# Local attention on blocks of 64 queries with their own 128 keys, on four 64x64 tiles of TensorE, in units of four heads

## The chip, the cores and the metric

The kernel runs on one core of one Trainium2 chip. The metric is the device time of the one launch in microseconds (us), from the first to the last instruction and what lies around them. PE is TensorE, PEld its weight loads, DVE is VectorE, ACT is ScalarE, POOL is GpSimd, SP is SyncE. PSUM is the memory that PE writes; it has 8 banks of 512 fp32 columns.

## The reference, cut to what matters

The model is a chain of stages over x of shape (2, 512, 128): a conditioned block (A, M), a quantised attention (B), a causal attention with an image key (C), and last a two-layer transformer (`_L0_ffn_ref`). Only the last has local attention, and only that is touched. Each of its 2 layers does, for 2 batches of 512 tokens, 8 heads of 64 channels and a window of 64:

```python
q = l2norm(q) * qs; k = l2norm(k) * ksc
q, k = rotary_xpos(q, k)
# local attention, w = n // 64 blocks of 64 queries, each with the keys of its own block and of the one before
bq = q.reshape(b, h, w, 64, d) * 8.0
bk, bv = look_around(bk), look_around(bv)          # (b, h, w, 128, d)
sim = einsum('bhwid,bhwjd->bhwij', bq, bk)
mask = (i < j) | (i > j + 64) | (j == -1)
attn = softmax(where(mask, -max, sim))
out = einsum('bhwij,bhwjd->bhwid', attn, bv)
x = x + out @ wo
```

After it come a shifted layer norm and a gated feed-forward part.

## The kernel before, in words

Everything is written out by hand in `build`, one program per engine, with named semaphores; the order of each engine's instructions is the order in the code, and there is no planner. Tokens are held in T = 8 tiles of 128 rows (TB = 4 per batch b). For each layer l the three projections are made tile by tile into `qkvD` (L1730, copied by ACT at L625). DVE takes the norms (L1209) and does the rotary part (`rope_terms`), for batch 0 ahead of the attention and for batch 1 inside the attention of batch 0: the generator `late_rope` (L1285 to L1290, and the scaling at L300) gives one piece of it in each unit of batch 0. `turn_qk(b)` (L1745) transposes q and k of one batch in 32 fp32 transposes; ACT (L619) and DVE (L278) copy them to `qTD` and `kTD`.

The attention itself goes in units of two heads (one `pair`) of one tile of 128 queries: 16 units per batch, 32 per layer, 64 in all. The 128 queries need up to 192 keys (the 64 before the tile, and its own 128), in a batch's first tile 128. A unit passes through the engines in this order:

- S on PE: two fp32 matmuls of 64x128 weights (the queries) and 192 columns (the keys), one for each head, in two row tiles (L1784), and on top of them two bf16 matmuls that add the mask (L1787). Each fp32 matmul is two instructions in the trace, and each fp32 transpose is one. The scores lie in banks 0 and 1 or 6 and 7.
- DVE: the negated maximum of both heads (`s_nmD`, L1319), its product with the scale (`s_nbD`, L1323), and, one unit behind, the reciprocal of the sums (`s_rsD`, L1332).
- ACT: one exponential per head with its sum (L653, two instructions each in the trace) into `prob_d(U)`, one of four buffers in `sq` and `dev`.
- POOL: both heads' probabilities times the reciprocals (L417).
- PE: four fp32 transposes of 128x128 (two in the first tile), L1803, two units behind S. The 64 columns of the first key tile that a query tile can't reach hold zeros, written once (L1222).
- ACT: the transposed probabilities copied to `probTD` (L666), also two units behind.
- PE: the product with the values, per head and key tile one fp32 matmul of 128x64 weights (values) and 128 columns, in two column tiles (L1820), three units behind S.
- DVE: `put_o`, once per tile, copies the output (L828).

PE's order in a unit u is S(u), transposes (u-2), values (u-3). S(u) waits until the exponentials of unit u-2 have left its banks. In batch 1 PE also runs `project_o` for the four tiles of batch 0 (L1753), one in each of its first four units, and `shift_rows` in unit 7; DVE runs `add_o` (unit 4), `receive` (7), `less_mean` (8) and `variance` (10), the layer norm of batch 0. At the seam between the batches PE runs `turn_qk(1)`.

## Time and profile before

| | |
|---|---|
| median of 3 runs | 843.0 us (842.24 to 846.91) |
| the profiled execution | 843.34 us, its span 841.4 us |
| mean granted TensorE clock | 0.813 |
| PE busy | 673.9 us (80%), 4514 instructions |
| DVE busy | 588.3 us (70%) |
| ACT busy | 520.9 us (62%) |
| POOL busy | 237.2 us (28%) |

An engine's busy share is a mean over stages with different limits, and matmuls overlap, so a busy PE is not PE at its peak. The granted clock is 1.0 at 2.4 GHz and 0.5 at 1.2 GHz. The four stretches of local attention (layer 0 and 1, batch 0 and 1) are the part to read: 555.5 to 594, 600 to 641, 716 to 754 and 760 to 801 us of the span.

### The profile page before, as it was taken

The page shows a single profiled execution, that of the slowest core. Times are in us where ns is not written, and L with a number is a line of the kernel's source. Part 1 is how long each engine was busy: PE and PEld are TensorE (multiplying, and loading weights), DVE is VectorE, ACT ScalarE, POOL GpSimd, SP SyncE. Part 2 cuts the span into 40 slices and gives each one's busy share as a digit, 9 for nine tenths or more (in the row PEclk, how much of TensorE's full clock was granted, in tenths as well). Part 3 has the DMA queues.
Part 4 walks back from the last instruction along what each step waited for, and adds up shares of the span by engine and source line. Part 5 has one row for each costly group of instructions (what it writes and reads, how often), then busy time and mean ns, then how long its engine had stood idle before and what let it go on. Part 6 is the DMA issues. An engine that isn't in the chain of part 4 may idle for free.

```text
span 841.4 us, 12993 instructions
## 1 busy us (share of the span) xinstructions
PE 673.9 (80%) x4514; PEld 406.8 (48%) x4514; DVE 588.3 (70%) x1285; ACT 520.9 (62%) x1237; POOL 237.2 (28%) x233
## 2 busy tenths in 40 slices
PE   6679976776889889858887887677898695779867
PEld 2322232542556556645554554254656543456545
DVE  7882348368998897577787764998454669874564
ACT  4479977654778777144776673745575475565742
POOL 5030040013889789512000000026231000452300
PEclk9689986888555555656999998969999797699998
DMA  9400000000000000000000000000000000000000
GB/s 296 142 1 1 2 2 0 1 0 1 1 2 1 1 2 1 1 0 1 1 2 1 2 2 0 1 0 1 2 2 1 0 1 1 0 2 1 1 1 25
DMA packets 9059, 10.54 MB, mean 13 GB/s; under 512 B 2746, under 2 KB 7844, under 8 KB 8868
## 3 DMA queue, kind: packets, MB, share of 16 engines
q1 hardware_dynamic: 8996, 9.73, 3.5%
q8 instruction: 36, 0.59, 0.3%
q14 instruction: 27, 0.22, 0.1%
HBM read 9.21 MB, written 0.52 MB: 12 GB/s over the span
## 4 chain that ended last, share of the span: by engine, by line
PE 45%; DVE 33%; ACT 9%; issue 8%; POOL 3%; DMA 0%; DVEq 0%; ACTq 0%; POOLq 0%
PE ps L1398 4%; PE ps L1561 4%; PE ps L1658 4%; DVE s_nmB L1040 3%; PE ps L1548 3%; PE ps L1641 3%; PE ps L1678 2%; DVE s_nmD L1319 2%; PE ps L1820 2%; PE ps L1803 2%; ACT arena L522 2%; PE ps L1839 2%; PE ps L1753 2%; PE ps L1469 2%; PE ps L1784 2%
## 5 line engine op out<-in xcount | busy, mean ns | idle before, releaser
L382 POOL TENSOR_SCALAR arena<-arena,s_rB,s_zpu 128x512 uint8<-128x512 f32 x128 | 115.9, 943 | 42.3 <-DVE s_rB L1013 41.5
L417 POOL TENSOR_TENSOR sq<-sq,s_rsD 128x384 f32<-128x384 f32 (+1 forms) x32 | 35.4, 1105 | 296.0 <-DVE s_rsD L1332 296.0
L560 ACT ACTIVATE arena<-ps,s_nmB 128x512 f32<-128x512 f32 x128 | 86.6, 683 | 31.4 <-DVE s_nmB L1040 30.8
L582 ACT ACTIVATE arena<-ps,s_nmx 128x512 f32<-128x512 f32 (+3 forms) x128 | 60.7, 527 | 49.7 <-DVE s_nmx L1138 49.3
L1040 DVE TENSOR_REDUCE s_nmB<-ps 128x2 f32<-128x1024 f32 x64 | 77.4, 1218 | 6.6 <-PE ps L1548 6.2
L1133 DVE TENSOR_REDUCE s_nmx<-ps 128x1 f32<-128x512 f32 (+3 forms) x128 | 56.6, 484 | 20.5 <-PE ps L1644 20.0
L522 ACT ACTIVATE arena<-ps 128x1024 f32<-128x1024 f32 x64 | 60.9, 1026 | 5.8 <-PE ps L1453 5.8
L1561 PE MATMUL ps<-cst,arena 128*128 128x128 f32 x256 | 61.9, 421 | 1.2 <-ACT arena L552 0.8
L1404 PE MATMUL ps<-ones 128*128 128x512 f16 x134 | 43.5, 488 | 22.2 <-ACT s_wn L493 6.6
L1319 DVE TENSOR_REDUCE s_nmD<-ps 128x2 f32<-128x384 f32 (+1 forms) x64 | 33.5, 524 | 39.1 <-PE ps L1787 28.9
L1561 PEld LDWEIGHTS ps<-cst,arena 128*128 128x128 f32 x256 | 49.3, 221 | 14.4 <-POOL arena L382 7.9
L1548 PE MATMUL ps<-staged 8*128 8x512 f16 x128 | 45.8, 580 | 12.4 <-ACT arena L560 11.5
L1658 PE MATMUL ps<-cst,arena 128*128 128x128 f32 x320 | 47.6, 303 | 8.6 <-issue 5.3
L653 ACT ACTIVATE sq<-ps,s_nbD,s_dq 128x192 f32<-128x192 f32 (+1 forms) x64 | 31.3, 493 | 32.3 <-DVE s_nbD L1323 32.3
L653 ACT ACTIVATE dev<-ps,s_nbD,s_dq 128x192 f32<-128x192 f32 (+1 forms) x64 | 31.3, 494 | 24.6 <-DVE s_nbD L1323 24.6
L1658 PEld LDWEIGHTS ps<-cst,arena 128*128 128x128 f32 x320 | 40.1, 157 | 11.8 <-issue 11.2
L417 POOL TENSOR_TENSOR dev<-dev,s_rsD 128x384 f32<-128x384 f32 (+1 forms) x32 | 32.3, 1010 | 47.2 <-DVE s_rsD L1332 47.2
L1730 PE MATMUL ps<-w_d,uT 128*128 128x512 f32 x96 | 42.3, 595 | 3.5 <-ACT uT L472 2.7
L1784 PE MATMUL ps<-arena 64*128 64x192 f32 (+1 forms) x256 | 39.7, 390 | 4.1 <-ACT sq L653 2.3
L1820 PE MATMUL ps<-arena 128*64 128x128 f32 x448 | 40.4, 296 | 1.7 <-ACT arena L666 1.4
L1641 PE MATMUL ps<-staged 51*128 51x512 bf16 (+3 forms) x128 | 32.7, 329 | 10.2 <-ACT arena L582 9.0
L1404 PEld LDWEIGHTS ps<-ones 128*128 128x128 f16 x134 | 14.8, 118 | 49.0 <-issue 13.0
(344 smaller groups left out, 1562.3 us busy)
## 6 DMA issues: line engine op xcount, KB each, us to landing
vec<-in_vec SPq DMA_DIRECT2D x1, 1882.0 KB, 11.9
w_d<-in_wqkv SPq DMA_DIRECT2D x2, 768.0 KB
vec<-in_vec SPq DMA_DIRECT2D x1, 960.0 KB, 8.3
w_h<-in_w SPq DMA_DIRECT2D x2, 341.0 KB
x_tok<-in_x SPq DMA_DIRECT2D x1, 512.0 KB, 4.1
arena<-in_w_f SPq DMA_DIRECT2D x2, 256.0 KB, 7.9
rope<-in_rope SPq DMA_DIRECT2D x1, 512.0 KB, 10.4
w_do<-in_wo SPq DMA_DIRECT2D x2, 256.0 KB
```

Source lines behind the costliest of these rows:

```text
L382: nc.gpsimd.tensor_scalar(u8[:, n % 4, j // 2, :, 2 * (j % 2)], prob[:, n % 2, j * 512:j * 512 + 512], sm("rB", 8)[:, c:c + 1], sm("zpu", ...
L417: nc.gpsimd.tensor_tensor(pr, pr, per_row(rs, 256 - k0), ALU.mult).then_inc(sem["normD"], 1)
L522: nc.scalar.activation(prob[:, n % 2, half * 1024:half * 1024 + 1024], ps[:, 2 * half:2 * half + 2, :], ACT.Exp, scale=HD ** -0.5).then_in ...
L560: nc.scalar.activation(prob[:, n % 2, j * 512:j * 512 + 512], ps[:, j, :], ACT.Exp, bias=sm("nmB", 8)[:, c:c + 1], accum_out=sm("sumB", 8) ...
L582: nc.scalar.activation(probC[:, n % 2, at(qt):at(qt) + w], ps[:, bank, col:col + w], ACT.Exp, bias=nmx[:, TB * b + qt, h:h + 1]).then_inc( ...
L653: nc.scalar.activation(prob_d(U)[:, j, k0:256], ps[:, 6 * (u % 2) + j, k0:256], ACT.Exp, scale=sm("dq8", 8 * T)[:, h:h + 1], bias=sm("nbD" ...
L1040: free(V.tensor_reduce(sm("nmB", 8)[:, c:c + 2], ps[:, 2 * half:2 * half + 2, :], X, ALU.max, negate=True), "maxB")
L1404: M(ps[:, 5, :], ones16[:, :], ones16[:, 0:1].to_broadcast([P, 512]), start=True, stop=True)
L1548: ins = M(ps[:, j, :], staged[r, G % 2, qt * P:qt * P + P], staged[r, G % 2, 512:1024], start=True, stop=True)
L1561: ins = nc.tensor.transpose(ps[:, 4 + i, c:c + P], codes[:, m % 4, i, c:c + P], ident)
L1641: M(o, stb[r, G % 2, qt * P:qt * P + P], stb[r, G % 2, 512:512 + w], start=(qt > 0), stop=False)
L1658: ins = nc.tensor.transpose(ps[:, 3 + bank, c:c + P], probC[:, n % 2, a:a + P], ident)
```

## The change

A unit is now four heads (two pairs) of one tile of 128 queries: 8 units per batch, 32 in all. Each half of the tile (64 queries) meets only its own 128 keys: the second half the keys of the tile, the first half the tile's first 64 keys and, in columns 64 to 127, the 64 keys before the tile. So each head has one square of 128x128 probabilities, and all of its rows are written.

- S: two bf16 mask matmuls of 256 columns come first, then eight fp32 matmuls of 64x64 weights and 128 columns, on four tiles of 64x64 (head j by half). In a batch's first tile the first half has 64 columns.
- DVE: one maximum, one product and one reciprocal per unit of four heads, over 4x128 columns. In batch 0 `late_rope` gives two pieces per unit, one before and one after the reciprocal.
- ACT: four exponentials of 128 columns, one copy of 512 columns.
- POOL: one product of 128x512, and a new step `mixed_values(l, t)` ahead of each tile: rows 0 to 63 of the tile's values, and rows 64 to 127 of the values of the tile before (not in a batch's first tile), are copied to the tile's q region of `qkvD`, which is dead by then. These are the weights for the first half.
- PE: four transposes, then eight fp32 matmuls of 128x64 weights and 64 columns for the values. A new wait on `mixD` stands ahead of them.
- `put_o`, `add_o`, `receive`, `less_mean`, `variance`, `squares_d` and `shift_rows` sit at other units; `project_o` runs for two tiles in each of the first two units of batch 1. The zeroing at L1222 is gone, and the mask table is another.

```diff
+                def s_d(b, u):
+                    t = TB * b + u // 2
+                    m = P * (u % (2 * TB) < 2)
+                    for j in range(2):
+                        M(ps[:, 6 * (u % 2) + j, 0:256], identb[:, :], dmask[:, m:m + P].unsqueeze(1).to_broadcast([P, 2, P]),
+                          start=True, stop=False)
+                    for a in range(2):
+                        for half in range(2):
+                            for j in range(2):
+                                r, pair = slice(64 * j, 64 * j + 64), 2 * (u % 2) + a
+                                q = qTD[r, pair, t * P + WINDOW * half:t * P + WINDOW * half + WINDOW]
+                                o = scores_d(u)[WINDOW * half:WINDOW * half + WINDOW, j, a, :]
+                                k = kTD[r, pair, t * P:t * P + P]
+                                if half == 0 and t % TB == 0:
+                                    o, k = o[:, 0:WINDOW], k[:, 0:WINDOW]
+                                elif half == 0:
+                                    k = kTD[r, pair, t * P - WINDOW:t * P + WINDOW].rearrange("p (n c) -> p n c", c=WINDOW)[:, ::-1, :]
+                                ins = M(o, q, k, start=False, stop=(a == 1))
+                    ins.then_inc(sem["sD"], 1)
+                def pv_d(t, v):
+                    for half in range(2):
+                        rows = slice(0, WINDOW if half == 0 and t % TB == 0 else P)
+                        for a in range(2):
+                            for j in range(2):
+                                pair, c = 2 * (v % 2) + a, P * (2 * j + a) + WINDOW * half
+                                values = 2 * INNER * half + DHD * (2 * pair + j)
+                                o = P * pair + WINDOW * half
+                                ins = M(ps[64 * j:64 * j + 64, 4 + t % 2, o:o + WINDOW], qkvD[rows, t, values:values + DHD],
+                                        probTD[rows, v % 2, c:c + WINDOW], start=True, stop=True)
+                    ins.then_inc(sem["pvD"], 1)
...
                         if u < TB * 2:
                             if u >= 2:
-                                pe.wait_ge(sem["expD"], 2 * (U - 1))
+                                pe.wait_ge(sem["expD"], 4 * (U - 1))
+                            s_d(b, u)
-                        if b == 1 and u < TB:
-                            project_o(u)
+                        if b == 1 and u < TB // 2:
+                            project_o(2 * u)
+                            project_o(2 * u + 1)
...
+            def mixed_values(l, t):
+                b = t // TB
+                pool.wait_ge(sem["qkT_D"], 8 * (B * l + b) + 4)
+                if T * l + t:
+                    pool.wait_ge(sem["normD"], 2 * (T * l + t))
+                step(nc.gpsimd.tensor_copy(qkvD[0:WINDOW, t, 0:INNER], qkvD[0:WINDOW, t, 2 * INNER:3 * INNER]), "mixD")
+                if t % TB:
+                    step(nc.gpsimd.tensor_copy(qkvD[WINDOW:P, t, 0:INNER], qkvD[WINDOW:P, t - 1, 2 * INNER:3 * INNER]), "mixD")
+                    for u in range(TB * 2):
+                        U = T * 2 * l + TB * 2 * b + u
+                        if u % 2 == 0:
+                            mixed_values(l, TB * b + u // 2)
+                        pool.wait_ge(sem["ratesD"], U + 1)
+                        rs = sm("rsD", 16)[:, 4 * (U % 4):4 * (U % 4) + 4]
+                        nc.gpsimd.tensor_tensor(prob_d(U), prob_d(U), per_row(rs, P), ALU.mult).then_inc(sem["normD"], 1)
...
-                            for j in range(2):
-                                c = 2 * (U % 4) + j
+                            for k in range(4):
+                                j, a = divmod(k, 2)
+                                c = 4 * (U % 4) + k
+                                nc.scalar.activation(prob_d(U)[:, k, :], scores_d(u)[:, j, a, :], ACT.Exp,
...
+                            step(V.tensor_reduce(nm, scores_d(u), X, ALU.max, negate=True))
+                            free(V.tensor_tensor(nb, nm, dq8[:, hh:hh + 4].rearrange("p (a j) -> p j a", j=2), ALU.mult),
+                                 "maxD")
+                        if b == 0 and u < TB * 2:
+                            next(rest, None)
                         if u >= 1:
-                            dve.wait_ge(sem["expD"], 2 * U)
+                            dve.wait_ge(sem["expD"], 4 * U)
+                            free(V.reciprocal(sm("rsD", 16)[:, c:c + 4], sm("sumD", 16)[:, c:c + 4]), "ratesD")
-                        if b == 0 and u < TB * 4:
+                        if b == 0 and u < TB * 2:
                             next(rest, None)
...
+                            for k in range(4):
+                                ins = nc.tensor.transpose(ps[:, 2 + u % 2, P * k:P * k + P], prob_d(U - 2)[:, k, :], ident)
                             ins.then_inc(sem["ptD"], 1)
...
+                            pe.wait_ge(sem["mixD"], 2 * (T * l + t) - (B * l + b) + 1)
+                            pv_d(t, u - 3)
```

## Rows read from the trace of the kernel before

**Rows 1.** Windows: stretch, then each engine's busy us (instructions), then granted clock, DMA

```profile
555.50:594.00 38.50, 29.63 (x224) 17.50 (x224) 31.78 (x69) 22.37 (x74) 20.29 (x14) 0.87 0.00 1
600.00:641.00 41.00, 36.27 (x329) 24.24 (x328) 19.97 (x64) 27.20 (x85) 13.19 (x17) 1.00 0.01 2
760.00:801.00 41.00, 36.35 (x329) 24.33 (x328) 20.06 (x64) 27.13 (x85) 13.19 (x17) 1.00 0.00 1
```

**Rows 2.** Timeline, PE, batch 1 of layer 0: start us, us, what, [idle before]

```profile
629.72 0.66 PE L1820 MATMUL ps<-arena 128*64 128x128 f32 x8
630.31 0.59 PE L1784 MATMUL ps<-arena 64*128 64x192 f32 x4
630.84 0.34 PE L1787 MATMUL ps<-dmask,identb 128*128 128x192 bf16 x2
631.01 0.60 PE L1803 MATMUL ps<-cst,dev 128*128 128x128 f32 x4
631.54 0.66 PE L1820 MATMUL ps<-arena 128*64 128x128 f32 x8
```

**Rows 3.** Timeline, batch 0 of layer 0: a rotary piece beside POOL's product

```profile
579.72 1.21 DVE L1290 TENSOR_TENSOR arena<-o_tok,staged 128x1024 f32<-128x1024 f32 x1
579.88 1.73 POOL L417 TENSOR_TENSOR sq<-sq,s_rsD 128x384 f32<-128x384 f32 x1 [2.10 <-DVE s_rsD L1332]
```

**Rows 4.** Groups by line and shape, batch 0 of layer 0, DVE: pieces of `late_rope`

```profile
L1285 DVE TENSOR_TENSOR o_tok<-arena,ropeL 128x1024 f32<-128x1024 f32 x4 | 4.8, 1207 | 0.0
L1288 DVE TENSOR_TENSOR staged<-arena,ropeL 128x512 f32<-128x512 f32 x4 | 4.4, 1090 | 0.1
L1287 DVE TENSOR_TENSOR staged<-arena,ropeL 128x512 f32<-128x512 f32 x4 | 2.7, 672 | 0.0
```

**Rows 5.** Timeline, PE: four column tiles; sixteen short matmuls with loads; both from other stages

```profile
98.56 1.07 PE L1469 MATMUL ps<-arena 128*32 128x512 f32 x8
303.09 0.59 PE L1575 MATMUL ps<-arena 128*128 128x5 f16 x16
```

**Rows 6.** Timeline, DVE, ACT, POOL, batch 1 of layer 0: one unit behind its scores

```profile
633.04 0.56 DVE L1319 TENSOR_REDUCE s_nmD<-ps 128x2 f32<-128x384 f32 x1 [0.98 <-PE ps L1787]
633.83 0.51 ACT L653 ACTIVATE dev<-ps,s_nbD,s_dq 128x192 f32<-128x192 f32 x1 [0.24 <-DVE s_nbD L1323]
633.95 0.82 POOL L417 TENSOR_TENSOR sq<-sq,s_rsD 128x384 f32<-128x384 f32 x1 [0.99 <-DVE s_rsD L1332]
634.82 0.59 ACT L666 ACTIVATE arena<-ps 128x512 f32<-128x512 f32 x1
634.93 0.60 PE L1803 MATMUL ps<-cst,sq 128*128 128x128 f32 x4
635.13 0.56 DVE L1319 TENSOR_REDUCE s_nmD<-ps 128x2 f32<-128x384 f32 x1 [1.26 <-PE ps L1787]
```

**Rows 7.** Groups by line and shape: instructions' total us, mean ns, idle before

```profile
L1133 DVE TENSOR_REDUCE s_nmx<-ps 128x1 f32<-128x512 f32 x32 | 22.0, 686 | 2.4 <-PE ps L1644 1.9
L653 ACT ACTIVATE dev<-ps,s_nbD,s_dq 128x128 f32<-128x128 f32 x16 | 7.2, 452 | 6.2 <-DVE s_nbD L1323 6.2
L407 POOL COPY arena<-arena 128x512 f32<-128x512 f32 x2 | 1.9, 938 | 0.0
L417 POOL TENSOR_TENSOR sq<-sq,s_rsD 128x256 f32<-128x256 f32 x2 | 1.2, 612 | 6.4 <-DVE s_rsD L1332 6.4
```

**Rows 8.** Timeline: the seam, and the start and end of batch 1

```profile
595.79 3.71 PE L1745 MATMUL ps<-cst,arena 128*128 128x128 f32 x32 [0.95 <-ACT dev L653]
603.19 0.49 PE L1784 MATMUL ps<-arena 64*128 64x128 f32 x4
640.97 0.71 PE L1753 MATMUL ps<-w_do,arena 128*128 128x128 f32 x4 [0.79 <-DVE arena L828]
```

**Rows 9.** Windows: the stretch at half clock; turning alone ahead of layer 1's attention

```profile
560.40:570.60 10.20, 9.07 (x44) 4.73 (x44) 8.29 (x18) 5.24 (x20) 5.23 (x4) 0.50 0.00 1
708.00:716.00 8.00, 6.66 (x36) 6.46 (x36) 7.79 (x11) 3.32 (x6) 0.00 (x0) 0.63 0.01 2
```

More of the change, by code:

```diff
@@ L638, in _ @@
                 for b in range(B):
-                    for u in range(TB * 4 + 2):
-                        U = T * 4 * l + TB * 4 * b + u
-                        if u == TB * 4 and b == 0:
+                    for u in range(TB * 2 + 2):
+                        U = T * 2 * l + TB * 2 * b + u
+                        if u == TB * 2 and b == 0:
                             turned_qk(1)
-                        if u < TB * 4:
-                            t, pair = divmod(u, 4)
-                            first = t == 0
+                        if u < TB * 2:
                             act.wait_ge(sem["maxD"], U + 1)
@@ L1219, in factors @@
                        d_.rearrange("p (t k h) -> p t k h", t=TB, k=2)[:, :, 0, :], 8.0, ALU.mult, name="d_dn")
-                for a in (wide["sq"], wide["dev"]) if l == 0 else ():
-                    step(V.memset(a[:, :, :].rearrange("p t c -> p (t c)").rearrange("p (n k) -> p n k", k=256)[:, :, 0:WINDOW],
-                                  0.0), "outside")
                 for t in range(TB):
@@ L1304, in _ @@
                 for b in range(B):
-                    for u in range(TB * 4 + 1):
-                        U = T * 4 * l + TB * 4 * b + u
-                        if u == TB * 4 and b == 0:
+                    for u in range(TB * 2 + 1):
+                        U = T * 2 * l + TB * 2 * b + u
+                        if u == TB * 2 and b == 0:
                             for i in (1, 3, 5, 7):
                                 turned_qk(1, i)
-                        if u < TB * 4:
-                            t, pair = divmod(u, 4)
-                            k0 = P if t == 0 else WINDOW
+                        if u < TB * 2:
@@ L1334, in _ @@
+                        if b == 0 and u < TB * 2:
                             next(rest, None)
-                        if u >= 8 and u % 4 == 0:
-                            put_o(l, TB * b + u // 4 - 2)
-                        if b == 1 and u == 4:
+                        if u >= 5 and u % 2:
+                            put_o(l, TB * b + (u - 5) // 2)
+                        if b == 1 and u == 2:
                             add_o(0)
-                        if b == 1 and u == 8:
+                        if b == 1 and u == 6:
@@ L1340, in _ @@
                             less_mean(0)
-                        if b == 1 and u == 10:
+                        if b == 1 and u == 7:
                             variance(0)
+                    put_o(l, TB * b + TB - 2)
                     put_o(l, TB * b + TB - 1)
@@ L1769, in _ @@
                     pe.wait_ge(sem["qk_evV"], 4 * (B * l + b + 1))
-                    for u in range(TB * 4 + 3):
-                        U = T * 4 * l + TB * 4 * b + u
-                        if u == TB * 4 and b == 0:
-                            pe.wait_ge(sem["expD"], 2 * U)
+                    for u in range(TB * 2 + 3):
+                        U = T * 2 * l + TB * 2 * b + u
+                        if u == TB * 2 and b == 0:
+                            pe.wait_ge(sem["expD"], 4 * U)
@@ L1782, in _ @@
                                 shift_rows(0)
-                            for j in range(2):
-                                M(ps[:, 6 * (u % 2) + j, k0:256], qTD[64 * j:64 * j + 64, pair, t * P:(t + 1) * P],
-                                  kTD[64 * j:64 * j + 64, pair, (t - 1) * P + k0:(t + 1) * P], start=True, stop=False)
-                            for j in range(2):
-                                ins = M(ps[:, 6 * (u % 2) + j, k0:256], identb[:, :], dmask[:, k0:256],
-                                        start=False, stop=True)
@@ L1795, in _ @@
                             pe.wait_ge(sem["normD"], U - 1)
-                            if l == 0 and U < 4:
-                                pe.wait_ge(sem["outside"], 2)
                             if U >= 4:
                                 pe.wait_ge(sem["ptcD"], U - 3)
-                            for j in range(2):
-                                for k in ((1,) if first else (0, 1)):
-                                    c = 256 * j + P * k
-                                    ins = nc.tensor.transpose(ps[:, 2 + v % 2, c:c + P],
-                                                              prob_d(U - 2)[:, j, P * k:P * k + P], ident)
+                            for k in range(4):
+                                ins = nc.tensor.transpose(ps[:, 2 + u % 2, P * k:P * k + P], prob_d(U - 2)[:, k, :], ident)
@@ L1812, in _ @@
                                 pe.wait_ge(sem["o_D"], T * l + t - 1)
[L1813 removed]
+                            if u % 2 and t == TB + 1:
                                 pe.wait_ge(sem["do_ev"], B * l + 1)
[L1815 to L1822 removed]
```

82 lines of the change are left out of this document (24 added, 58 removed).

## The prediction

> **What bounds the kernel now.** I read the table of busy shares first; it names PE, but over all stages. So next the windows over the stretches the change touches. Batch 0 of layer 0 takes 38.5 us with PE busy for 29.6 and DVE for 31.8, batch 1 takes 41.0 us with PE busy for 36.3 and DVE for only 20.0 [rows 1]. Layer 1 repeats layer 0 (its batch 1 is the last line of [rows 1]), so each sum is made for layer 0 and doubled. The reader is to see two different limits, and the timeline shows both.
>
> In batch 1 PE runs unit after unit with hardly a gap: values 0.59 us from start to start, scores 0.53, mask 0.17, transposes 0.53, in all 1.82 us for two heads [rows 2]. PE sets the pace. In batch 0 DVE does the rotary part besides: four pieces each of L1285 (1.21), L1287 (0.67), L1288 (1.09) and of the addition at L1290 (1.21), and two scalings at L300, taken at the same 1.2, together 19.1 us [rows 3, 4]. POOL's product, 0.82 us alone, lasts 1.73 when it starts 0.16 us after such a piece [rows 3, 6]: it waits until the piece is over. DVE, POOL and PE take turns there.
>
> **PE's work for a unit of four heads.** 32 transposes of 128 columns take 3.71 us from first start to last end [rows 8], so one each 0.11 us. Four of them last 0.53 until the next kind starts [rows 2], which is 4 x 0.11 and 0.09 for the change to another tile shape. The value matmuls (eight instructions in two column tiles) take 0.59, which is four rounds of 0.11, 0.06 for the first weights and 0.09 for the change: two tiles do run beside each other. Scores are two rounds of 192 columns (0.16), the weights of 128 columns (0.11) and the change (0.09), 0.52.
> - Scores after: 16 instructions of 128 columns. If four tiles of 64x64 run beside each other it is four rounds of 0.11, 0.05 for weights, 0.09 for the change: 0.58. The trace before has no tile of 64 rows and 64 columns. The nearest is L1469, four column tiles of 32: eight instructions of 512 columns in 1.07 us, so only two rounds [rows 5]. Nothing overlapping would be 16 x 0.11 = 1.8 plus 0.14, 1.9; more overlap than one round for four isn't to be had. I take 0.58, and 1.9 for the range.
> - Values after: eight rounds of 64 columns, 0.055 each, 0.06 and 0.09: 0.59 against 2 x 0.59. 16 matmuls with their loads come out in 0.59 us, less the last one's 0.17 or so, that is 0.027 each [rows 5], so the issue of 16 takes 0.43 and doesn't slow the 0.44.
> - Mask: 2 x 256 columns at 0.107, and a change of tile shape ahead of the scores: 0.30. Transposes: four instead of eight, 0.53.
> The sum is 2.00 us instead of 3.64.
>
> A rule that speaks against the value part: the Trainium skill (TensorE: Matmul & The Clock Gate, Part 3, "The mechanism") says that a weight load overlaps a running matmul only where the row group differs. All value matmuls use all rows. By it each of eight loads of about 0.05 us would be exposed, 0.4 us a unit, and the result would be about 818 us. The row speaks against it: eight loads and eight passes fit in 0.59 us, of which the columns alone take 0.44 [rows 2].
>
> **The other engines, for four heads.** ACT: four exponentials of 128 columns, 0.45 each [rows 7], and one copy (0.59, the next starts 0.49 after): 2.3 us, before 4 x 0.49 and two copies, 2.9. DVE: the maximum of 512 columns costs 0.69 (L1133 [rows 7]) and the two small ones 0.08 each from start to start, with the gaps 0.91; before twice 0.75. POOL: 256 columns 0.61, 384 columns 0.82 [rows 6, 7], so 512 take 1.04. The mixed values are new: two copies of 64x512 per tile, one per unit. The nearest row is L407, 128x512 at 0.94 [rows 7]; the bounds are 0.4 (half of that, if fewer rows cost less) and 2.1 (0.94 and a whole rotary piece waited for). I take 0.94. The new wait on `mixD` stands on PE ahead of the values; behind it are the next scores. The copies end three units earlier, so it costs nothing.
>
> **Batch 1 after.** POOL needs 1.98 a unit, PE 2.00, ACT 2.3; none of them sets the pace, a round trip does. From a maximum to the first exponential 0.79 [rows 6], plus 0.13 for the longer maximum; four exponentials until the copy may start 1.79; the copy of the earlier unit 0.59 and 0.05; then PE values 0.59, mask 0.30, scores 0.49, and 0.20 until the maximum two units on starts (634.93 to 635.13 [rows 6]). That is 4.93 us for two units, 2.46 each. The trip over POOL is shorter: 1.04 to its start, 1.04 there, 0.05, transposes 0.53, then the same 1.58: 4.24. So what ends last moves from PE's columns to the copy that stands behind four exponentials in ACT's queue.
> Before, batch 1 runs from 603.19 to the projection at 640.97 [rows 8], 37.8 us. After: in each of the first two units scores (0.88) and 16 instructions for two tiles of `project_o` (16 x 0.11, 0.09), 2.75 each; the transposes of unit 0 start at 6.4, of unit 1 at 8.7, of unit 7 at 8.7 + 6 x 2.46 = 23.5; its copy, values and `put_o` end 2.8 later, 26.3. The layer norm of batch 0 on DVE and the shift on PE, now in half as many units, add 1.5. So 27.8 us, 10.0 less.
>
> **Batch 0 after.** DVE has 7 units of 0.91, the 19.1 us of rotary pieces (14 in 16 places, so they end in unit 6) and one `put_o` of 0.7: 26.2 us. The copies on POOL hold back a piece by some 0.4 each, as L1288 (1.09) is held against L1287 (0.67), the same size [rows 4]: 2.8. So 29.0 us for seven units, 4.1 each. The trip over POOL with a piece ahead of the reciprocal is 4.24 + 1.3 + up to 1.0 of waiting = 6.5 for two units at the full clock, some 8.4 at half clock, so it ties with DVE there. The first maximum is about 1.2 us after the start at 555.9; with the last exponentials (2.7) `turn_qk` starts at 589.0 instead of 595.79, 6.8 less. Against that stand longer units at the seam (0.5) and some loss to the clock (1.0). So 5.3 less. The zeroing at L1222 lay in DVE's idle time: 0.
>
> **Sum.** 2 x (10.0 + 5.3) = 30.6 us off the profiled execution's 843.34 (span 841.4), which is 0.3 over the median of 843.0: **813 us**.
>
> **Rivals.**
> 1. The clock. PE does less in batch 0: 2.0 us of work in 4.1. It was already at half clock (1.2 GHz) from 560.4 to 570.6, where it waited for DVE and POOL in the first units [rows 9], and at 2.4 GHz afterwards. If it stays at half for the whole of batch 0, a unit is about 4.5 us (2.5 more) and `turn_qk(1)` starts at half (2.5 more): 5 per layer, 823 us. For it: fewer columns in the same time. Against it: the work comes in dense bursts. The Trainium skill (TensorE: Matmul & The Clock Gate, Part 4) has it that transposes don't count as busy for the clock. The trace disagrees: PE ran transposes alone ahead of layer 1's attention, at a mean of 0.63 over 8 us [rows 9], so the clock rose on them. By the rule, the 2.0 us would count as only 1.5, and this rival would be the likelier; by the row I hold it back.
> 2. The four tiles don't all run together. In pairs the scores cost 0.44 more: 2 to 3 us per layer, 818. One after another 1.3: the trip is 3.1 a unit, 6 to 7 per layer, 826.
> 3. Slower. Each change between tiles of a different row and column drains, 0.11 + 0.09 for each of 16 passes: scores 3.2, PE 4.6 a unit. Batch 1 would take 8 x 4.6 and some 6, 43 us against 37.8, and batch 0, twice that slow in its half-clock part, about 10 more: 2 x 15, 873 us. It decides from the point where a unit costs 3.9 us in batch 1, that is scores of 2.5. Against it: pairs of row tiles and of column tiles run without a drain [rows 2].
> 4. Better. The copies on POOL fall where DVE reads PSUM and hold nothing back (2.5), and ACT's 2.3 sets batch 1 (1.3), with the seam and clock free (1.5): 5.3 per layer, 802.
>
> **How the numbers follow.** The forecast has 0.57, the clock 0.16, the tiles without overlap 0.12, slower 0.04, better 0.11. 813 is that of the likeliest. The range goes down to rival 4's 802 and a little past it, 801, and up to 829: past the clock (823) and serial tiles (826), and it holds the copies at 2.1 (about 2 per layer, 817); what is left out is rival 3, two rivals together, and a mis-sized trip. Faster by over 0.5% (about what a measurement tells from no change) 0.94, within it 0.02, slower 0.04.
>
> **What would show it.** In batch 1 a unit of 2.4 to 2.5 us, with the value matmuls waiting for ACT's copy (L666's successor) and PE idle for 0.4 of it; the sixteen score passes in 0.6 us; batch 1 of 28 us, batch 0 of 33. The first product on POOL about 1.04 alone, and a copy of mixed values near 0.9. Wrong would be: PE still without gaps in batch 1 (rival 2), a clock of 0.5 at the seam (rival 1), POOL as what transposes wait for in batch 1 (the copies cost more than 1.4), or stretches outside the attention that move by more than 1 us.

## The result, and the profile after

The changed kernel takes **817.8 us** (median of 4 runs, 816.6 to 818.8) against 843.3 for the kernel before on the same chip: a ratio of 0.9697 (95% interval 0.9664 to 0.9731), 25.5 us less. Forecast were 813 and 801 to 829. The profiled execution has a span of 816.3 us (841.4 before) and a mean granted clock of 0.780 (0.813 before). One run of e2 below (1021.1 us) was a slow one: e2's median of 809.3 counts it, its ratio does not, and the other five have a median of 808.2.

The windows show the three stretches of layer 0 that the prediction's sum is made of; the fourth line is a part of batch 1. Columns as in [rows 1].

```profile
557.50:590.20 32.70, 21.05 (x249) 13.77 (x249) 27.84 (x47) 18.31 (x71) 17.13 (x13) 0.68 0.01 2
590.20:599.60 9.40, 8.39 (x94) 7.50 (x98) 3.83 (x7) 3.97 (x7) 2.13 (x3) 0.85 0.01 2
599.60:630.00 30.40, 25.30 (x340) 18.65 (x341) 15.49 (x38) 20.84 (x75) 12.44 (x14) 0.89 0.01 1
610.10:616.90 6.80, 6.80 (x60) 4.65 (x58) 0.95 (x3) 4.01 (x16) 2.79 (x4) 0.50 0.00 0
```

The reader is to see the granted clock, the last number but two: 0.68, 0.85 and 0.89, where batch 0 stood at 0.87 and batch 1 at 1.00 before [rows 1]. In 6.8 us in the middle of batch 1 TensorE was busy without a break at half clock (1.2 GHz). The stretches at half clock are 562.3 to 582.8, 589.6 to 593.0 and 610.1 to 616.9; before, only 560.4 to 570.6 in this part of layer 0 [rows 9], and 720.8 to 734.5 in layer 1. In the changed kernel layer 1 has the same three: 709.1 to 729.6, 736.4 to 739.8, 756.9 to 763.7.

The timeline of PE in batch 1, first at full clock, then at half, then at full again (start, us, what, idle before and who ended it); it answers to [rows 2]:

```profile
604.80 0.38 PE L1774 MATMUL ps<-dmask,identb 128*128 128x256 bf16 x2
605.11 0.67 PE L1787 MATMUL ps<-arena 64*64 64x128 f32 x16
605.71 0.66 PE L1826 MATMUL ps<-cst,sq 128*128 128x128 f32 x4
...
608.00 0.66 PE L1826 MATMUL ps<-cst,sq 128*128 128x128 f32 x4 [0.82 <-POOL sq L431]
609.17 0.83 PE L1799 MATMUL ps<-arena 64*64 64x64 f32 x16 [0.52 <-ACT arena L675]
...
610.36 1.13 PE L1787 MATMUL ps<-arena 64*64 64x128 f32 x16
611.42 1.11 PE L1826 MATMUL ps<-cst,dev 128*128 128x128 f32 x4
612.46 1.32 PE L1799 MATMUL ps<-arena 64*64 64x64 f32 x16
...
617.57 0.69 PE L1799 MATMUL ps<-arena 128*64 128x64 f32 x16
618.19 0.39 PE L1774 MATMUL ps<-dmask,identb 128*128 128x256 bf16 x2
618.51 0.67 PE L1787 MATMUL ps<-arena 64*64 64x128 f32 x16
619.81 0.66 PE L1826 MATMUL ps<-cst,sq 128*128 128x128 f32 x4 [0.63 <-POOL sq L431]
620.92 0.69 PE L1799 MATMUL ps<-arena 128*64 128x64 f32 x16 [0.46 <-ACT arena L675]
```

Sixteen score passes take 0.60 us from their start to the next kind's (605.11 to 605.71), values 0.62 (617.57 to 618.19), the mask 0.31. At half clock the scores take 1.06 (610.36 to 611.42). Where [rows 2] has no gap, PE now waits: ahead of the transposes for Pool's product (0.82, 0.63, 0.57 and 0.21 us in batch 1), ahead of the values for ScalarE's copy (0.52, 0.46, 0.57 and 0.46).

The other sizes, by shape over 557 to 630 (count, total us, mean ns, idle before); they answer to [rows 6, 7]:

```profile
L1321 DVE TENSOR_REDUCE s_nmD<-ps 128x4 f32<-128x512 f32 x16 | 11.0, 690 | 13.8 <-PE ps L1787 7.3 <-ACT sq L665 3.7 <-issue 1.4
L675 ACT ACTIVATE arena<-ps 128x512 f32<-128x512 f32 x16 | 9.5, 601 | 3.0 <-PE ps L1826 3.0
L420 POOL COPY arena<-arena 64x512 f32<-64x512 f32 x7 | 5.7, 810 | 0.9
L422 POOL COPY arena<-arena 64x512 f32<-64x512 f32 x6 | 5.6, 933 | 0.4
```

And one copy of mixed values beside a rotary piece, with the product that follows it on Pool; the product at 604.15, in batch 1, is one by itself ([rows 3] has such a pair of before):

```profile
570.30 1.22 DVE L303 TENSOR_TENSOR arena<-o_tok,s_dn 128x1024 f32<-128x1024 f32 x1
570.41 1.58 POOL L420 COPY arena<-arena 64x512 f32<-64x512 f32 x1
572.05 1.50 POOL L422 COPY arena<-arena 64x512 f32<-64x512 f32 x1
573.62 1.04 POOL L431 TENSOR_TENSOR dev<-dev,s_rsD 128x512 f32<-128x512 f32 x1
...
604.15 1.04 POOL L431 TENSOR_TENSOR sq<-sq,s_rsD 128x512 f32<-128x512 f32 x1 [6.24 <-DVE s_rsD L1334]
```

The seam answers to [rows 8]: the turn of queries and keys, the first scores of batch 1, and the projection that ends it.

```profile
590.15 5.10 PE L1748 MATMUL ps<-cst,arena 128*128 128x128 f32 x32 [0.66 <-ACT dev L665]
...
599.19 0.39 PE L1774 MATMUL ps<-dmask,identb 128*128 128x256 bf16 x2
...
629.77 3.84 PE L1756 MATMUL ps<-w_do,arena 128*128 128x128 f32 x32 [0.79 <-DVE arena L837]
```

Where the time went, layer 0, from first starts on PE. The stretches, in the order of the columns: `turn_qk(0)` to `turn_qk(1)` is batch 0; to the first `project_o` is the seam; to the fifth `project_o` is batch 1; to layer 1's `turn_qk(0)` is all that lies between the attentions. The experiments stand in the same table.

```
kernel                          batch 0   seam   batch 1   between
before                            47.1     8.3     36.9      67.5
after                             39.5    10.0     29.7      67.2
e1  extra matmuls                 37.6     8.6     27.0      66.8
e2  no mixed values               38.8     8.6     26.6      66.6
e3  copy early                    39.5    10.0     28.5      69.1
e4  other order of tiles          39.7     9.9     29.8      67.1
e5  e1 + matmuls ahead            37.6     8.6     27.0      68.4
e7  units of two heads            46.6     8.7     36.1      69.3
e8  before + extra matmuls        45.6     8.3     37.1      66.5
e9  e7 + extra matmuls            43.7     8.6     36.7      67.5
e10 e1 without mixed values       36.9     9.7     26.8      66.8
e11 e1 + copy early               37.6     8.6     28.5      69.0
e12 e1 + scores twice             37.6     9.6     31.4      67.5
e13 e11, last unit as it was      37.6     8.6     27.5      66.8
```

Batch 0 is 7.6 us shorter, the seam 1.7 longer, batch 1 7.2 shorter, what lies between 0.3 shorter: 13.4 in layer 0.

Layer 1 is not always a copy of layer 0, since the clock can fall elsewhere in it. The same stretches for it (the fourth column goes to the end of the span), and in the last column when layer 0's `turn_qk(0)` starts, in us from the start of the span:

```
kernel                          batch 0   seam   batch 1   to the end   first turn
before                            47.4     8.3     36.9      40.4         548.7
after                             39.5    10.2     29.6      40.1         550.6
e1  extra matmuls                 37.6     8.6     27.0      39.5         548.3
e2  no mixed values               38.5    10.2     29.2      40.4         546.0
e8  before + extra matmuls        45.2     8.3     37.1      39.1         548.8
e9  e7 + extra matmuls            43.4     7.5     33.1      42.1         549.0
e10 e1 without mixed values       36.9     9.6     26.8      39.5         549.8
```

The first turn starts between 545.5 and 551.0 us in the fourteen profiles, although next to nothing ahead of it differs (e5's matmuls, the zeroing that the change removes): up to 5.5 us of a single profile's difference has nothing to do with an edit, and a price is safer read from the stretches.

### The profile page after: what moved, and what is told of

It is laid out like the page before. It is cut to its first block, busy times and chain, and to the rows that moved or that the text cites. A ratio compares the mean times of both kernels' runs of the same rounds, so it can differ in the third digit from the quotient of the medians.

```text
span 816.3 us, 13070 instructions
## 1 busy us (share of the span) xinstructions
PE 644.8 (79%) x4674; PEld 394.5 (48%) x4674; DVE 571.1 (70%) x1187; ACT 500.2 (61%) x1205; POOL 234.1 (29%) x229
## 4 chain that ended last, share of the span: by engine, by line
PE 44%; DVE 32%; ACT 12%; issue 8%; POOL 3%; DMA 0%; POOLq 0%; ACTq 0%; DVEq 0%
PE ps L1401 5%; PE ps L1564 4%; PE ps L1661 4%; DVE s_nmB L1049 3%; PE ps L1551 3%; PE ps L1644 3%; ACT arena L536 3%; PE ps L1681 2%; PE ps L1472 2%; PE ps L1748 2%; PE ps L1853 2%; PE ps L1444 2%; DVE s_nmD L1321 2%; PE ps L1389 2%; DVE s_dss L1218 1%
## 5 line engine op out<-in xcount | busy, mean ns | idle before, releaser
L420 POOL COPY arena<-arena 64x512 f32<-64x512 f32 x16 | 12.5, 784 | 240.8 <-PE ps L1748 239.0
L1142 DVE TENSOR_REDUCE s_nmx<-ps 128x1 f32<-128x512 f32 (+3 forms) x128 | 56.6, 483 | 20.5 <-PE ps L1647 20.0
L1564 PE MATMUL ps<-cst,arena 128*128 128x128 f32 x256 | 61.9, 422 | 1.2 <-ACT arena L566 0.8
L1661 PE MATMUL ps<-cst,arena 128*128 128x128 f32 x320 | 47.6, 304 | 8.6 <-issue 5.3
L665 ACT ACTIVATE sq<-ps,s_nbD,s_dq 128x128 f32<-128x128 f32 x64 | 28.4, 454 | 31.2 <-DVE s_nbD L1325 31.2
L1321 DVE TENSOR_REDUCE s_nmD<-ps 128x4 f32<-128x512 f32 x32 | 22.1, 690 | 27.5 <-PE ps L1787 14.6
L431 POOL TENSOR_TENSOR sq<-sq,s_rsD 128x512 f32<-128x512 f32 x16 | 22.5, 1404 | 55.2 <-DVE s_rsD L1334 55.1
L1748 PE MATMUL ps<-cst,arena 128*128 128x128 f32 x128 | 23.0, 362 | 19.2 <-DVE arena L303 17.8
L665 ACT ACTIVATE dev<-ps,s_nbD,s_dq 128x128 f32<-128x128 f32 x64 | 28.5, 457 | 15.7 <-DVE s_nbD L1325 15.7
L1472 PE MATMUL ps<-arena 128*32 128x512 f32 x256 | 35.6, 630 | 1.0 <-ACT arena L536 1.0
```

What stands on the lines that cost most here:

```text
L665: nc.scalar.activation(prob_d(U)[:, k, :], scores_d(u)[:, j, a, :], ACT.Exp, scale=sm("dq8", 8 * T)[:, h:h + 1], bias=sm("nbD", 16)[:, c:c ...
L1142: ins = V.tensor_reduce(nmx[:, TB * b + qt, h:h + 1], ps[:, bank, col:col + P * (qt + 1)], X, ALU.max, negate=True)
L1564: ins = nc.tensor.transpose(ps[:, 4 + i, c:c + P], codes[:, m % 4, i, c:c + P], ident)
L1661: ins = nc.tensor.transpose(ps[:, 3 + bank, c:c + P], probC[:, n % 2, a:a + P], ident)
```

## The experiments

Twelve kernels, each timed in 5 rounds (e4 in 3) beside the kernel before, whose medians were 842.9 to 843.8. Theory: the time that the forecast missed is the clock; the trip through the engines sets the pace. Rivals: the work itself, the copies, the tiles.

**e1: extra matmuls where TensorE waits.** They write a PSUM bank that the transposes then overwrite; 64 in batch 0 and 16 in batch 1 of a layer. The wait for Pool's product (`normD`) moves behind them.

```diff
+def warm(u, n):
+    for _ in range(n):
+        M(ps[:, 2 + u % 2, 0:256], ones16[:, :], ones16[:, 0:1].to_broadcast([P, 256]), start=True, stop=True)
...
+    if b == 0 and u < 2:
+        warm(u, (0, 10)[u])
...
+    warm(u, (24, 6, 6, 6, 6, 6, 0, 0)[u - 2] if b == 0 else 2)
     pe.wait_ge(sem["normD"], U - 1)
```

> The changed kernel with extra bf16/f16 matmuls of ones (256 columns each, results never read) put on TensorE where it waits in the attention: 10 and 24 in the first units of batch 0, six in each later unit of batch 0, two in each of batch 1. They keep the granted clock up. My theory: what the change fell short of my 813 us is the clock (0.5 in 20 us of batch 0, at the seam, and in 7 us of batch 1 of each layer). Then the clock is 1.0 through both batches, batch 0 takes 30 instead of 32.7 us, the turning at the seam 3.7 instead of 5.1, batch 1 27.5 instead of 30.4: 5 to 6 us per layer, about 807 us (804 to 811). Rival: VectorE and GpSimd set the pace of batch 0 anyway, and the extra matmuls stand in the way of real ones: 816 to 820.

Measured **803.3 us** (ratio 0.9553, 0.9523 to 0.9584): 14.5 less than the change, more than the theory asked for. The windows of the three stretches have a clock of 1.00 throughout:

```profile
555.00:585.60 30.60, 22.54 (x312) 15.45 (x312) 28.27 (x47) 18.14 (x70) 16.95 (x13) 1.00 0.01 2
585.60:593.40 7.80, 6.45 (x86) 5.87 (x88) 3.54 (x6) 4.27 (x9) 2.44 (x3) 1.00 0.01 2
593.40:621.40 28.00, 24.61 (x366) 17.93 (x360) 15.57 (x37) 20.75 (x75) 12.44 (x14) 1.00 0.01 2
```

In layer 0 it gains 2.0 us in batch 0, 1.3 at the seam, 2.7 in batch 1 and 0.5 after: 6.4; in layer 1 6.6. That is 13.0 us of the 15.3 by which the two profiled spans differ; the other 2.3 lie ahead of the first turn, where nothing was changed. Work that computes nothing made the kernel faster, and the clock is what it got back.

**e8: the same in the kernel before,** in batch 0 alone (56 matmuls a layer, `warm(u, 6)` in the second unit, then 12, 8, 5, 4, 3 and 2 ahead of the transposes).

> The kernel before the change, with matmuls of 256 columns of ones (f16, result thrown away) issued where TensorE waits in batch 0. Theory (the clock's loss comes with the change: before, only 560.4 to 570.6 stood at half clock in batch 0 of a layer): little is to be had, at most what those 10.2 us lose per layer, 2 to 3 us each: 838 (835 to 842). Rival (the extra matmuls are worth as much to any kernel of this shape, 14.5 us as in e1_warm): 828 to 830.

Measured 837.4 (0.9917, 0.9884 to 0.995), as the theory said. So the extra matmuls are worth 5.5 us to the kernel before (5.5 by the stretches too) and 14.5 to the changed one (13.0 by the stretches). With both held at full clock in the attention the change is worth 34.1 us (837.4 to 803.3); 25.5 were seen.

**e2: without the mixed values.**

```diff
-    if u % 2 == 0:
-        mixed_values(l, TB * b + u // 2)
...
-    pe.wait_ge(sem["mixD"], 2 * (T * l + t) - (B * l + b) + 1)
-    values = 2 * INNER * half + DHD * (2 * pair + j)
+    values = 2 * INNER + DHD * (2 * pair + j)
```

> The changed kernel without the copies of mixed values on GpSimd (both halves use the tile's own values, so the first half's output is another). My theory: the copies hold back rotary pieces on VectorE and the next product on GpSimd in batch 0 only, 2 to 3 us per layer: 812 us (810 to 814). Rival 1: they lie wholly in GpSimd's idle time: 817 to 818. Rival 2: they also delay batch 1: 808 or less.

Measured 809.3 (0.9613, 0.9576 to 0.965), 8.5 less: it seemed to confirm a price. But in its trace batch 1 of layer 0 has a clock of 1.00:

```profile
557.00:578.50 21.50, 15.64 (x157) 10.45 (x158) 18.88 (x31) 11.42 (x46) 9.11 (x5) 0.53 0.00 2
578.50:590.00 11.50, 8.00 (x109) 6.70 (x108) 8.12 (x16) 7.69 (x23) 3.54 (x3) 1.00 0.01 1
590.00:620.00 30.00, 24.39 (x377) 18.26 (x377) 15.54 (x39) 21.30 (x76) 8.78 (x9) 1.00 0.01 2
```

Layer 1 is the better comparison, since its seam and batch 1 have nearly the clock of the changed kernel (0.83 and 0.88 against 0.84 and 0.88; batch 0 0.72 against 0.67): there the edit wins 1.0 us in batch 0 and 0.4 in batch 1, and 1.0 in the whole layer. Layer 0 wins 5.8, of which 4.5 stand at the seam and in batch 1, where the clock rose. The remaining 4.6 us of this profile (spans 816.3 and 805.0) lie ahead of the first turn.

**e10: the same edit on top of e1,** meant to have the same clock in both.

> e1_warm without Pool's copies of the mixed values and the wait on them (the value matmuls of the first 64 queries of a tile then read unmixed values: that part of the output is left wrong). e2_no_mixed took the copies from the changed kernel and gained 8.5 us, but its granted clock rose with it. Theory (most of those 8.5 us were the clock; at full clock the copies cost what they delay, 1 to 2 us a layer): 800 (797 to 802). Rival (the copies themselves cost 4 us a layer, whatever the clock): 794 to 796.

Measured 804.3 (0.953, 0.9504 to 0.9557) against e1's 803.3: no difference. Both expectations fell by the number. By the stretches, in either layer, batch 0 is 0.7 shorter, batch 1 0.3 shorter and the seam 1.0 longer, because 3.4 us of it stood at half clock again: the clock was not the same after all, and took back what the edit won. Both experiments thus put the copies on Pool at some 1 us a layer, 2 of e2's 8.5; the rest was the clock in layer 0 and time ahead of the attention.

**e4: the four passes of a tile behind one another,** not two (one matmul) of each tile in turn.

```diff
-    for a in range(2):
-        for half in range(2):
-            for j in range(2):
+    for half in range(2):
+        for j in range(2):
+            for a in range(2):
```

> The changed kernel with the two score matmuls of one 64x64 tile one after the other, so that neighbours in the queue share a tile instead of going round the four. My theory: the gain of the scores rests on going round the tiles; in this order the sixteen passes take about 1.5 us instead of 0.6, a unit of batch 1 goes from 2.5 to about 3, and batch 0 loses as much: 832 us (826 to 838). Rival: the order in the queue doesn't matter, because passes to free tiles overtake: 817 to 819.

Measured 816.2 (0.9701, 0.9663 to 0.9739): my theory fell. In its timeline the sixteen passes take 0.62 us to the next start, as in the change's own order, 0.60:

```profile
619.71 0.69 PE L1787 MATMUL ps<-arena 64*64 64x128 f32 x16
620.33 0.66 PE L1826 MATMUL ps<-cst,sq 128*128 128x128 f32 x4
```

The four tiles of 64x64 overlap in either order, with two or with four passes of the same tile next to each other.

**e7: the squares of 64 queries, in units of two heads.** Lines are cut to the pattern; DVE's side work (`add_o`, the layer norm of batch 0, `put_o`) keeps its order but stands in units twice as many.

```diff
-    for u in range(TB * 2 + 2):
-        U = T * 2 * l + TB * 2 * b + u
+    for u in range(TB * 4 + 2):
+        U = T * 4 * l + TB * 4 * b + u
...
-    return ps[:, 6 * (u % 2):6 * (u % 2) + 2, 0:256].rearrange("p j (a k) -> p j a k", k=P)
+    return ps[:, 6 * (u % 2):6 * (u % 2) + 2, 0:P]
...
-    for k in range(4):
+    for j in range(2):
```

> One half of the change alone: squares of 128x128 probabilities on 64x64 tiles, but in units of two heads as before (16 units per batch). My theory: work per head is that of the changed kernel, but the trip of a unit has fixed parts, so that two heads take 1.5 us and four heads 3.0 instead of 2.46; batch 1 gets 2 to 4 us longer than in the changed kernel, batch 0 1 to 2: 824 us (820 to 829). Rival A: the squares alone bring all of it: 817. Rival B: the units of four bring all of it: 838 or more.

Measured 845.2 (1.0037, 1.0015 to 1.0058): rival B by the number, nothing at all is left of the gain. But its clock is 0.57 in batch 0 and 0.79 in batch 1, so this number alone says little about units. **e9** adds extra matmuls to it (6, then 14, 10, 6, 5 and 4 a unit in batch 0, one in batch 1).

> e7_two_heads (squares of 64 queries, but units of two heads) with extra matmuls of 256 columns where TensorE waits, some 6 to 14 in the first units and 4 in later ones of batch 0, 1 in batch 1. Theory (e7's 27 us against the change are largely the half clock that its sparse TensorE gets over nearly all of batch 0): 822 (815 to 829). Rival (they are the trip from engine to engine, made 16 times instead of 8 per batch, each at its fixed prices): 838 to 845.

Measured 830.2 (0.9852, 0.9818 to 0.9887): between the two, nearer to the theory's edge of 829 than to the rival's 838. The windows of e7's batches in layer 0, then of e9's, with batch 1 of its layer 1 as the third line, then batch 1 of e8:

```profile
557.50:595.20 37.70, 31.11 (x272) 17.06 (x272) 28.97 (x65) 19.16 (x78) 22.91 (x21) 0.54 0.01 1
603.00:639.90 36.90, 32.76 (x360) 20.96 (x356) 17.84 (x61) 22.15 (x83) 14.00 (x22) 0.80 0.01 2
```

```profile
557.50:592.90 35.40, 30.78 (x355) 19.84 (x355) 29.22 (x66) 19.78 (x78) 22.89 (x21) 0.93 0.01 2
601.50:638.20 36.70, 33.71 (x363) 21.93 (x363) 16.83 (x60) 22.21 (x83) 13.99 (x22) 0.81 0.01 2
756.41:789.51 33.10, 29.17 (x362) 19.28 (x362) 17.08 (x60) 22.01 (x82) 14.02 (x22) 1.00 0.01 2
```

```profile
602.77:639.84 37.07, 32.81 (x294) 22.24 (x294) 18.34 (x60) 26.01 (x83) 12.37 (x16) 1.00 0.01 1
```

So with extra matmuls in all three, squares alone bring 7.2 us (837.4 to 830.2) and the larger unit 26.9 (830.2 to 803.3), but the clock blurs this split. In layer 0 e9's batch 1 takes 36.7 us at a clock of 0.81; the same batch of layer 1, at 1.00, takes 33.1. At full clock batch 1 thus goes from 37.1 (e8) to 33.1 by the squares and to 27.0 (e1) by the larger unit: 4.0 and 6.1. If layer 0 of e9 ran as its layer 1 does, the kernel would be 5.0 us faster; by that estimate the squares are worth some 12 of the 34.1 us and the larger unit some 22, and what lies behind e9's attention still stands at a lower clock than in e1. Where e9's side work stands was my choice, which I did not vary. Pool's busy time shows one part of the difference: 22.9 us in batch 0 with 21 instructions, 17.0 with 13 in e1.

**e12: mask and scores of batch 1 issued twice,** on top of e1.

```diff
-def s_d(b, u):
+def s_d(b, u, again=False):
...
+    if b == 1 and not again:
+        return s_d(b, u, True)
     ins.then_inc(sem["sD"], 1)
```

> e1_warm with mask and scores of each unit of batch 1 issued twice (the second group starts the accumulation anew, so the output stays): 0.88 us more of TensorE per unit, on the trip. Theory (the trip through the engines sets batch 1, two units to a trip, so a unit grows by half of 0.88): 3.5 us a layer, 810 (808 to 813). Rival A (TensorE's queue sets it: a unit grows by all of 0.88): 7 us a layer, 816 to 819. Rival B (the work hides in TensorE's waits): 803 to 805.

Measured 815.5 (0.9656, 0.9627 to 0.9685). From the first mask to the last unit's is 24.17 us (593.49 to 617.66) against 19.69 (593.57 to 613.26) in e1, so a unit grows by 4.48 / 7 = 0.64 us on average, to 3.45 from 2.81. A second mask and scores take 0.93 (614.44 to 615.37), a little more than the 0.88 expected. Neither rule holds alone, and the average hides it: from mask to mask the seven units last 2.81, 2.80, 1.58, 3.56, 3.49, 2.29 and 3.16 us in e1 and 3.73, 3.72, 2.50, 3.56, 4.23, 3.21 and 3.22 here. Four of them pay in full, one in most, two nothing. With the unit at the seam and the tail layer 0 grows by 6.1 us; the total of 12.2 is nearer to rival A (816 to 819) than to the theory. In the timeline PE has no wait left in the middle of the batch; the last line is the last unit's first mask:

```profile
613.83 0.69 PE L1801 MATMUL ps<-arena 128*64 128x64 f32 x16
614.44 0.39 PE L1774 MATMUL ps<-dmask,identb 128*128 128x256 bf16 x2
614.76 0.67 PE L1787 MATMUL ps<-arena 64*64 64x128 f32 x16
615.37 0.39 PE L1774 MATMUL ps<-dmask,identb 128*128 128x256 bf16 x2
...
617.66 0.39 PE L1774 MATMUL ps<-dmask,identb 128*128 128x256 bf16 x2
```

**e3: ScalarE's copy of the turned probabilities behind the second exponential,** in batch 1.

```diff
+    if b == 1 and k == 1 and u >= 2:
+        copy_turned(U, u)
...
-    if u >= 2:
+    if u >= 2 and (b == 0 or u >= TB * 2):
+        copy_turned(U, u)
```

> The changed kernel with ScalarE's copy of the turned probabilities issued after the second of the four exponentials of a unit in batch 1, not behind the fourth. Theory (the trip sets the pace of batch 1, and the copy stands at its late end, TensorE waiting for it 20 times, 10.8 us): values start up to 1.1 us earlier per unit, TensorE gains some 0.3 to 0.5 us in 7 units of 2 layers: 812 (809 to 815). Rival (the third and fourth exponential come later by the copy's 0.66 us, so Pool's product, the transposes and the next copy do too, and nothing is won): 817 to 820.

Measured 818.6 (0.9708, 0.9677 to 0.974). That is the rival's number. Batch 1 became 1.2 us shorter, and what lies behind it 1.9 longer, with the clock at half from 624.1 to 634.3. **e11** puts it on e1.

> e1_warm with ScalarE's copy of the turned probabilities behind the second exponential in batch 1, as in e3_copy_early, where batch 1 took 28.45 us instead of 29.66 but the projection behind it and the stages after ran at half clock and gave it back. Theory (at full clock the gain stays: 1 us or so per layer): 801 (799 to 803). Rival (the exponentials behind the copy are later by it, and nothing is won): 803 to 806.

Measured 813.8 (0.9639, 0.961 to 0.9669): 10 us slower than e1, and worse than both expectations. The last unit's mask begins 18.7 us after the first (19.7 in e1), but the exponentials of the last unit are put off by the copy, PE waits in the tail, and the clock falls:

```profile
617.17 0.66 PE L1840 MATMUL ps<-cst,dev 128*128 128x128 f32 x4 [1.58 <-POOL dev L431]
...
619.67 1.11 PE L1840 MATMUL ps<-cst,dev 128*128 128x128 f32 x4 [0.79 <-POOL dev L431]
```

**e13** leaves the last unit as it was and fills the tail's waits with 8 matmuls a unit.

> e11_warm_early (813.76) lost 10 us to e1_warm although its last scores of batch 1 began 19.4 us after the first, against 20.4. This kernel moves ScalarE's copy between the exponentials only where another unit follows (not in the last unit, whose exponentials it put off), and has eight extra matmuls instead of two in each of the last two units, where TensorE waited 1.6 and 0.8 us and the granted clock then fell to half from 618.8 to 629.0. Theory (the loss was those two things, the gain of 1 us a layer is real): 801 (799 to 804). Rival (a copy between the exponentials wins nothing at the end of the batch even so, or the denser steady part is followed by a half clock anyway): 808 to 814.

Measured 806.5 (0.9549, 0.9518 to 0.958); its six runs lie at 798.5 and 800.8 and four times at 806.2 to 807.0, so it is not told apart from e1. The profiled one (800.8) has a batch 1 of 27.5 us, e1 27.0: the loss of e11 was the tail and the clock (the two edits were not tried one by one), but an earlier copy wins nothing. In its trace the last unit's scores start at 609.80 and make way for PE's next work at 610.40, but their maximum starts at 611.45, behind two operations of the layer norm on VectorE:

```profile
609.80 0.67 PE L1793 MATMUL ps<-arena 64*64 64x128 f32 x16
610.15 0.54 DVE L731 TENSOR_SCALAR s_s<-s_s 128x4 f32<-128x4 f32 x1
610.40 0.39 PE L1812 MATMUL ps<-ones 128*128 128x256 f16 x2
610.72 0.69 DVE L1263 TENSOR_TENSOR o_tok<-x,s_s 128x512 f32<-128x512 f32 x1
611.45 0.69 DVE L1327 TENSOR_REDUCE s_nmD<-ps 128x4 f32<-128x512 f32 x1
```

In e1 those two are over when its scores are; the time won on ScalarE is waited for on VectorE.

**e5: 28 more matmuls ahead of `turn_qk(0)`,** on top of e1.

> e1_warm with 28 more idle matmuls ahead of the first turn of queries and keys of a layer, where the granted clock was at half from 542.7 to 552.9 and TensorE waits. Theory: that turn and the first unit run at full clock, 1 to 2 us per layer: 800 (798 to 803). Rival (the turn waits for the rotation on VectorE and ScalarE anyway, whatever the clock): 803 to 805.

Measured 804.7 (0.9536, 0.9508 to 0.9565): the rival. The clock was full from 517 to 638, and the turn of layer 0 still took 6.1 us from its first to its last transpose, as at half clock. It waits for the rotary part (L303) and for copies out of PSUM (L278):

```profile
548.88 2.40 PE L1751 MATMUL ps<-cst,arena 128*128 128x128 f32 x20 [1.39 <-DVE arena L303]
552.86 1.09 PE L1751 MATMUL ps<-cst,arena 128*128 128x128 f32 x8 [1.58 <-DVE arena L278]
554.58 0.66 PE L1751 MATMUL ps<-cst,arena 128*128 128x128 f32 x4 [0.63 <-DVE arena L278]
```

In layer 1 the turn took 4.5 us instead of 6.1, but it also began 1.6 later, behind the extra matmuls. A full clock won nothing where TensorE was not what ended last. By its median e1 is the fastest version found; it beats the change by 14.5 us.

## Why the prediction came out right, step by step

**TensorE's work for a unit.** Right. Scores 0.60 (0.58 forecast), values 0.62 (0.59), mask 0.31 (0.30). The rule in the Trainium skill (TensorE: Matmul & The Clock Gate, Part 3, "The mechanism") that loads overlap only across row groups does not hold for the values: sixteen loads and sixteen passes of 64 columns on all rows fit in 0.62 us, although a load lasts 0.13 to 0.14 us in the profile.

**The other engines.** Right: the maximum 0.69, the product 1.04 alone. The copies of mixed values were forecast at 0.94 within bounds of 0.4 and 2.1; measured 0.60 to 0.61 by themselves and 1.50 to 1.65 beside rotary pieces. That they cost 0.4 a piece in batch 0, 2.8 us in all, was too much: without them batch 0 is 0.7 shorter (e10).

**Batch 1: 27.8 us forecast, 30.6 measured** (599.19 to 629.77) by the points of [rows 8]. This is the term that was mis-sized, and by the clock: e1 at 1.00 needs 27.93 (593.57 to 621.50). I had priced the clock for batch 0 and the seam only, and none for batch 1, where 6.8 us at 0.50 stood in the middle. But the parts of the 27.8 were off against each other. The two units with the projection are right (2.81 and 2.80, 2.75 forecast). The other five last 2.82 on average in e1, not 2.46, and between 1.58 and 3.56: there is no steady pace. Some of the 0.4 may be VectorE's side work and the shift, which I had as a lump of 1.5; no run separates it.

**That the trip replaces PE as what ends last.** Half right. PE does wait for ScalarE's copy, 0.46 to 0.57 us at a time, as forecast. But it waits as much for Pool's product (0.82, 0.63, 0.57, 0.21), which I had named as a sign that the copies cost more than 1.4; the copies take 0.60 to 1.09 each there, only the wait of 0.57 (at 624.94) comes right behind two of them, and without them batch 1 is 0.3 shorter (e10). What makes Pool's product late was not tried. And e12 shows that PE's queue is close behind: four of seven units pay in full for more work on PE. The reading of the kernel before, that PE sets the pace of batch 1, holds in part: with PE's passes cut and the number of trips kept, batch 1 goes from 37.1 to 33.1 at full clock (e8, and e9's layer 1). The squares cut ScalarE's work too (26.0 to 22.0 us busy in these windows), so the 4.0 are not shown to be PE's alone. e7 (36.1 at 0.79) and e9's layer 0 (36.7 at 0.81) hide this behind the clock. The other 6.1, to 27.0, come with half as many trips that carry twice the heads.

**Batch 0: `turn_qk` 6.8 us earlier, less 1.5 for seam and clock: 5.3.** Measured 7.6 from turn to turn, less 1.7 at the seam: 5.9. Right in sum, in part by luck: the copies were priced at 2.8 and cost 0.7, the clock at 1.0 and it cost 2.0 in batch 0 and 1.3 at the seam. Half clock lasted 20.5 us in batch 0 and cost only 2.0 (e1); VectorE, busy for 28.3 of 30.6 us in e1, leaves little room there. The terms as written give a turn at 588.8, not 589.0, a slip of 0.2.

**The rivals.** The clock (823) came true in kind, with its sign, half clock at the seam: in layer 0 it cost 6.4 us (e1), 2.0 in batch 0, 1.3 at the turn, 2.7 in batch 1 and 0.5 behind it. Its 5 a layer was a whole batch 0 and the turn at half clock; what came was 20.5 us of batch 0, the turn, and 6.8 us of batch 1, which it had not named. Tiles that don't overlap: excluded by the 0.60. Slower through drains: excluded by the same row. Better (802) is what e1 reached, through the clock, and not through ACT's pace or Pool's copies.

**The sum.** The forecast's 813 kept the clock's losses of the kernel before (5.5 us, e8) and added 2.0; its work at full clock was thus 805.5 us. The runs have 803.3 for the work (e1) and 14.5 for the clock instead of 7.5 (13.0 by the stretches alone). So the work was right within some 2 us, and the clock's term was about half of what it is. By stretches the change brings 13.4 us in layer 0 and 13.7 in layer 1, 27.0 against the 30.6 forecast; the spans show 25.1, because this profile's first attention began 1.9 later than in the profile of before (557.9 and 555.9). That start varies by itself: in e4, whose instructions ahead of it are the same, it is 555.5. A start that moves by over 1 us was among the signs of being wrong; here it tells nothing about the change.

## What to carry over

When a change takes work from TensorE and leaves it waiting, read the granted clock of each stretch in the new profile before pricing anything else: here holding it up was worth 5.5 us before the change and 14.5 after it. Compare variants stretch by stretch and only where the clock is the same in both (a few useless matmuls where TensorE waits can make it so, but look: in e10 they did not at the seam), or a cost of some 2 us will be read as 8.5, as in e2. Look at both layers: e9's layer 1 showed what its layer 0 hid. And count trips through the engines, not only columns: at full clock a unit twice as large was worth 6.1 us in batch 1, the smaller squares 4.0.

## What the runs showed of the hardware

- 80 matmuls of ones per layer, none of whose results is used, saved 14.5 of 817.8 us, 1.8%. The Trainium skill (TensorE: Matmul & The Clock Gate, Part 1, "What's actually happening") advises that for modelling the ramp penalty is under 1% of a typical kernel's span. That is said of the clock's rise. Here the clock fell again in each batch, and that cost more, 13.0 us by the stretches, and decided between versions.
- The clock was at half while TensorE had no gap (6.80 us busy of 6.80, 610.1 to 616.9); its waits lay just ahead, at 608.00 (0.82 idle) and 609.17 (0.52 idle). A slow stretch need not look idle itself.
- Sixteen f32 passes of 128 columns on four tiles of 64x64 take 0.60 us with two passes of a tile in turn and 0.62 with four (e4), with a change of tile shape ahead of and behind them.
- A copy of 64x512 on Pool between two places in SBUF is 0.60 by itself and 1.50 to 1.65 beside a VectorE operation with two SBUF inputs. The Trainium skill (GPSIMD Engine Reference, section 1, "Specifications") has it that such operations contend for the shared interface; the trace agrees.
